# Counting two blocks of nodes with one pass over the edges, in the first stage of a graph network kernel

## The chip, the cores and the metric

The kernel runs on one core of a Trainium2 chip. The metric is the device time of one execution in microseconds (us), the median of several. Its engines are TensorE (PE, with its weight loads as PEld), VectorE (DVE), ScalarE (ACT), GpSimd (POOL) and SyncE (SP). Each runs its own instruction queue, and they wait for each other on semaphores.

## The reference

The reference is four graph layers over the same 400,000 edges between 12,500 nodes. Each layer normalises the node rows, gathers rows by edge, and adds the messages up by one end of the edge:

```python
h = relu(layernorm(x));  x = x + relu(segment_sum((h @ W0[r])[src, type] * w, dst))          # layer 0
h = relu(layernorm(x));  x = x + update(h, segment_sum(relu([h[src], e64] @ M + b), dst))    # layer 1
h = relu(layernorm(x));  x = x + segment_sum((h @ W2[r])[src, type], dst)                    # layer 2
h = relu(layernorm(x));  x = x + mlp_norm(h + segment_sum(h[dst] + e16 @ We + be, src))      # layer 3
```

Nothing in it asks for an order of the edges. The kernel needs one: it sorts edges by blocks of 128 nodes, by destination for three layers and by source for the last. To know where each block begins, it must first count the edges of each block.

## The kernel before

The 12,500 nodes make NB = 98 blocks of 128. The 400,000 edges lie on 128 partitions, COLS = 3125 per partition. The kernel is a chain of ten stages with a barrier of all engines between any two (`end_stage`). The first stage, `starts_stage`, is the only one that the change touches. It finds, for each of the 98 destination blocks and 98 source blocks, where the block's edges begin. Its work:

- SyncE loads `src` and `dst` (`ints`, `key`). VectorE shifts both by 7 bits (lines 289 and 293) and writes the block numbers as bf16 into `keys`. There the two kinds alternate, so that `k3[:, :, 0]` is the destination block and `k3[:, :, 1]` the source block, each at a step of two elements.
- VectorE then fills small constant tiles (lines 298 to 311), among them `pad`, and SyncE writes 212 filler tiles to `rec` and `rec2` (lines 224 and 227), on its own queue.
- The counts per partition go to `cnt`, 196 wide. VectorE counts destination blocks 0 to DV - 1 = 85 directly, one pass over the 3125 edges for each (line 314): compare with the block's number, and add the ones up in the accumulator output. After each pass it waits for its own semaphore.
- ScalarE counts the rest by signs. One pass (line 247) sums the sign of `number of the block - key` shifted by a half, and the difference of two neighbouring sums is twice a count. It makes 98 passes for the source blocks, then 12 for destination blocks 86 to 97 (line 253), each waiting for the one before.
- VectorE goes on with the remainders of the node numbers (lines 317 to 323, six operations over all edges), waits for ScalarE's last sum, takes the differences (lines 326 and 327), halves them (line 328) and releases TensorE (`s_cnt`).
- TensorE sums the counts over partitions (lines 263 and 264), VectorE makes tile numbers of them, and at `s_last` SyncE and ScalarE each write 49 padding tiles (line 211) through their queues. The stage ends when those have landed. Meanwhile VectorE and TensorE compute the lists `blks` and `blkd` (lines 360 to 366).

The next stage, `record_stage`, begins behind the barrier.

Of the kernel before, what the change touches and what calls it, by code (L numbers as in the profile page):

```python
# [14 lines left out]
BF16 = mybir.dt.bfloat16  # L15
I32 = mybir.dt.int32
ALU = mybir.AluOpType
ACT = mybir.ActivationFunctionType
# [8 lines left out]
NB = -(-N // P)  # L27
COLS = E // P
# [36 lines left out]
KEYS = 2  # L65
# [2 lines left out]
EQ = 3 * P  # L68
EW = EQ + CG * FE
WIDE = KEYS * NB  # L70
DV = 86
SPARE = -(-NB // G)


def peeled(engine, count, step):

    step(0)
    with engine.Fori(1, count) as i:
        step(i)


def wait_earlier(engine, semaphore, value):

    if not isinstance(value, int) or value > 0:
        engine.wait_ge(semaphore, value)
# [30 lines left out]
def build(nc, a, out):  # L116
    ctx = ExitStack()
    with ctx:
# [22 lines left out]
        keys, off, padq = b.take(COLS, BF16), b.take(WIDE), b.take(QT * ROW // 2, BF16)  # L141
        lasts = b.take(2 * NB, I32)
        starts_stage(nc, sem, a, Buffers(arena, b.at), psum, iotaf, ident, iotab, identb, ones, pidx, epsc, blkd, blks,
                     ints, flts, srcl, keys, off, padq, lasts, rec, rec2)
        sem.end_stage()
# [29 lines left out]
def starts_stage(nc, sem, a, b, psum, iotaf, ident, iotab, identb, ones, pidx, epsc, blkd, blks,  # L175
# [3 lines left out]

    key, tmp = b.take(COLS, I32), b.take(COLS, I32)  # L180
    eq, junk = (b.take(COLS // 2 + 1, BF16)[:, 0:COLS] for _ in range(2))
    tri, nums, nbias = b.take(P), b.take(NB + 1), b.take(NB + 1)
    gd, gs = b.take(NB + 1), b.take(NB + 1)
    cnt, tiles, incl, ti, wide = (b.take(WIDE) for _ in range(5))
    ti = ti.bitcast(I32)
    col = [b.take(1) for _ in range(KEYS)]
# [12 lines left out]
    s_v, s_ks, s_kd, s_hist, s_sign, s_cnt, s_pre, s_last, s_tge, s_tps, s_blk = (  # L199
        sem("r_" + n) for n in ("v", "ks", "kd", "hist", "sign", "cnt", "pre", "last", "tge", "tps", "blk"))  # L200
    k3 = keys.rearrange("p (t k) -> p t k", k=KEYS)
    TC, QC = ([(c, min(512, n - c)) for c in range(0, n, 512)] for n in (TILES, QUADS))

    def pad_last_tiles(engine, lo, hi, at):

        with engine.Fori(lo, hi) as i:
            engine.load(at, last[0:1, bass.ds(i * 2, 2)])
            group = engine.snap(at[0], min_val=0, max_val=GROUPS + SPARE - 1)
            place = engine.snap(at[1], min_val=0, max_val=G - 1)
            tile = rect[bass.ds(group, 1), bass.ds(place, 1)].rearrange("g j p w -> (g j p) w")  # L210
            engine.dma_start(tile, pad).then_inc(s_filled, 16)

    with nc.Block() as block:
        @block.sync
        def _(sp):
            sp.dma_start(ints[:, COLS:2 * COLS], a["src"]).then_inc(s_src, 16)
            sp.dma_start(key, a["dst"]).then_inc(s_dst, 16)
            sp.dma_start(flts[:, 0:COLS], a["w"]).then_inc(s_rest, 16)
            sp.dma_start(ints[:, 0:COLS], a["type"]).then_inc(s_rest, 16)

            sp.wait_ge(s_pad, 1)
            with sp.Fori(FULL, GROUPS) as g:
                for j in range(G):
                    sp.dma_start(rect[bass.ds(g, 1), j:j + 1].rearrange("g j p w -> (g j p) w"), pad).then_inc(s_fill, 16)
            with sp.Fori(FULL, GROUPS2) as g:
                for j in range(G // QT):
                    sp.dma_start(quads[bass.ds(g, 1), j:j + 1].rearrange("g j p w -> (g j p) w"), padq).then_inc(s_fill, 16)
            sp.wait_ge(s_fill, FILLS * 16)
            at = [sp.alloc_register(f"r_last{k}") for k in range(2)]
            sp.wait_ge(s_last, 1)  # L230
            pad_last_tiles(sp, 0, NB // 2, at)
            sp.wait_ge(s_filled, NB * 16)
# [8 lines left out]
        @block.scalar  # L241
        def _(act):
            act.wait_ge(s_ks, 1)

            def source_signs(i):
                wait_earlier(act, s_sign, i)
                nc.scalar.activation(junk, k3[:, :, 1], ACT.Sign, bias=nbias[:, bass.ds(i, 1)],
                                     accum_out=gs[:, bass.ds(i, 1)]).then_inc(s_sign, 1)
            peeled(act, NB, source_signs)
            act.wait_ge(s_kd, 1)  # L250
            with act.Fori(DV, NB) as i:
                act.wait_ge(s_sign, i + (NB - DV))
                nc.scalar.activation(junk, k3[:, :, 0], ACT.Sign, bias=nbias[:, bass.ds(i, 1)],
                                     accum_out=gd[:, bass.ds(i, 1)]).then_inc(s_sign, 1)
            at = [act.alloc_register(f"r_lasta{k}") for k in range(2)]
            act.wait_ge(s_last, 1)
            act.wait_ge(s_fill, FILLS * 16)
            pad_last_tiles(act, NB // 2, NB, at)
# [18 lines left out]
        def _(dve):  # L277
            chain = [0]

            def link(ins):  # L280
                chain[0] += 1
                ins.then_inc(s_v, 1)
                dve.wait_ge(s_v, chain[0])

            v = nc.vector
# [18 lines left out]
            link(v.memset(epsc, EPS))  # L304
            link(v.memset(ones, 1.0))
            link(v.memset(gs[:, NB:NB + 1], -float(COLS)))
            link(v.memset(gd[:, NB:NB + 1], -float(COLS)))
            link(v.tensor_scalar(ident, iotaf, pidx, None, ALU.is_equal))
            link(v.tensor_copy(iotab, iotaf))
            link(v.tensor_copy(identb, ident))  # L310
            link(v.tensor_scalar(tri, iotaf, pidx, None, ALU.is_gt))
            dve.wait_ge(s_kd, 1)
            with dve.Fori(0, DV) as i:
                v.tensor_scalar(eq, k3[:, :, 0], nums[:, bass.ds(i, 1)], None, ALU.is_equal, ALU.add,
                                accum_out=cnt[:, bass.ds(i, 1)]).then_inc(s_hist, 1)
                dve.wait_ge(s_hist, i + 1)
            link(v.tensor_scalar(tmp, key, P - 1, None, ALU.bitwise_and))
            link(v.tensor_copy(flts[:, COLS:2 * COLS], tmp))
            link(v.tensor_scalar(tmp, ints[:, COLS:2 * COLS], P - 1, None, ALU.bitwise_and))
# [2 lines left out]
            link(v.tensor_scalar(tmp, ints[:, COLS:2 * COLS], 4, None, ALU.logical_shift_left))  # L322
            link(v.tensor_tensor(ints[:, 0:COLS], tmp, ints[:, 0:COLS], ALU.bitwise_or))

            dve.wait_ge(s_sign, NB + NB - DV)
            link(v.tensor_tensor(cnt[:, DV:NB], gd[:, DV:NB], gd[:, DV + 1:NB + 1], ALU.subtract))
            link(v.tensor_tensor(cnt[:, NB:WIDE], gs[:, 0:NB], gs[:, 1:NB + 1], ALU.subtract))
            v.tensor_scalar(cnt[:, DV:WIDE], cnt[:, DV:WIDE], 0.5, None, ALU.mult).then_inc(s_cnt, 1)
            dve.wait_ge(s_pre, 1)

            quantum = (P, QT * P)
# [1126 lines left out]
```

## Time and profile before

| what | value |
|---|---|
| median of 3 runs | 23065.33 us (23064.5 to 23086.5) |
| the profiled execution | 23081.41 us |
| its span, first to last instruction | 23079.6 us |
| busy in the span: GpSimd, VectorE, TensorE, ScalarE | 67%, 44%, 41%, 8% |
| VectorE's counting passes (line 314) | 86, 298.6 us busy |
| ScalarE's counting passes (lines 247 and 253) | 110, 2.902 us each |
| first instruction of the second stage | at 465.1 us |

The busy shares are means over ten stages. The change lies in the first, which takes 2% of the span. There GpSimd is idle but for 3.5 us, so the shares of the whole say nothing of this stage.

### The profile page before, as it was taken

The numbers are of one execution on the slowest core, as the hardware profiler recorded it, in microseconds if no ns is written. First come the engines' busy times: TensorE is split into PE (matmuls) and PEld (weight loads), VectorE is DVE, ScalarE is ACT, GpSimd is POOL, SyncE is SP. The second block draws the span as 40 slices with busy tenths as digits, with TensorE's granted clock in tenths as the row PEclk, the third lists the DMA queues.
The fourth block names the chain that finished last, engine by engine and source line by source line (L and its number), as shares of the span: only waits on it lengthen the run. The fifth ranks groups of instructions, "written<-read, shape, count | busy, mean of one in ns | idle before, by whom it ended". The sixth has DMA issues, their size and how long they took to land. (4 is left out here: it accounts for less than half of the span.)

```text
span 23079.6 us, 208272 instructions
## 1 busy us (share of the span) xinstructions
PE 9435.0 (41%) x48147; PEld 7205.3 (31%) x48150; DVE 10242.7 (44%) x25180; ACT 1861.0 (8%) x4901; POOL 15540.0 (67%) x16453
## 2 busy tenths in 40 slices
PE   0777776433333334333333543333332222222366
PEld 0333333233333333333333333333331111111254
DVE  7777777544444443333333432222224333333473
ACT  5000000000000000000000100000001111111100
POOL 0777777777777767777777267777776777777400
PEclk8555555555555555555555655555555555555686
DMA  2333332222222232222222322222223222222462
GB/s 86 99 98 98 99 98 81 70 64 61 64 61 62 63 45 62 61 63 61 61 61 61 72 89 63 61 64 61 64 61 64 83 83 83 83 82 82 131 222 69
DMA packets 1005113, 1785.47 MB, mean 77 GB/s; under 512 B 352294, under 2 KB 461123, under 8 KB 1004534
## 3 DMA queue, kind: packets, MB, share of 16 engines
q1 hardware_dynamic: 484294, 1127.71, 15.6%
q0 software_dynamic: 513696, 654.80, 12.5%
q10 hardware_dynamic: 7056, 2.21, 0.0%
q8 instruction: 24, 0.39, 0.0%
q14 instruction: 43, 0.35, 0.0%
HBM read 1279.37 MB, written 510.79 MB: 78 GB/s over the span
## 5 line engine op out<-in xcount | busy, mean ns | idle before, releaser
L1018 PE MATMUL psum<-arena 128*128 128x64 f32 x19392 | 4447.2, 424 | 7925.5 <-DMA arena<-table,arena 4589.6
L919 POOL DMA_INDIRECT arena<-table,arena x6464 | 6104.2, 944 | 2005.8 <-issue 1932.5
L1018 PEld LDWEIGHTS psum<-arena 128*128 128x128 f32 x19392 | 4226.9, 330 | 8146.0 <-issue 6208.1
L970 DVE TENSOR_TENSOR arena<-arena,psum 128x64 f32 x9696 | 2150.5, 222 | 6333.8 <-PE psum L1018 4413.8
L687 POOL DMA_INDIRECT rec<-arena x3125 | 3001.1, 960 | 1476.0 <-issue 949.0
L1123 POOL DMA_INDIRECT rec<-arena x3232 | 3180.4, 984 | 1093.8 <-issue 971.1
L919 POOL DMA_INDIRECT arena<-ptable,arena x3232 | 3147.6, 974 | 997.8 <-issue 984.3
L464 PE MATMUL psum<-arena 128*128 128x196 bf16 (+1 forms) x4375 | 1378.5, 429 | 1262.4 <-DVE arena L595 1262.3
L1142 DVE TENSOR_TENSOR arena<-psum,arena 128x1024 bf16<-128x1024 f32 x404 | 494.6, 1224 | 2716.2 <-DMA arena<-rec 2716.2
L1190 PE MATMUL psum<-arena 128*128 128x128 bf16 x3232 | 418.0, 311 | 2526.8 <-DVE arena L1142 2526.8
L1190 PEld LDWEIGHTS psum<-arena 128*128 128x128 bf16 x3232 | 312.7, 141 | 2673.6 <-DVE arena L1142 2345.0
L595 DVE TENSOR_TENSOR arena<-psum,arena 128x392 f32<-128x392 f32 x1875 | 918.2, 490 | 365.1 <-PE psum L464 241.0
L464 PEld LDWEIGHTS psum<-arena 128*128 128x128 bf16 x4375 | 366.8, 115 | 2188.1 <-DVE arena L595 1812.4
L949 DVE TENSOR_TENSOR arena<-psum,arena 128x1024 f32<-128x1024 f32 x808 | 984.1, 1218 | 25.7 <-issue 22.6
L976 DVE TENSOR_TENSOR arena<-arena 128x512 f32<-128x512 f32 x404 | 287.4, 711 | 1580.5 <-DMA arena<-ptable,arena 1580.5
L1201 PE MATMUL psum<-arena 128*128 x3232 | 589.6, 363 | 643.0 <-DVE arena L1150 552.8
L1291 PE MATMUL psum<-arena 128*128 128x81 bf16 x10560 | 604.2, 228 | 471.8 <-DVE arena L1259 465.8
L600 DVE TENSOR_REDUCE arena<-arena 128x10 f32<-128x980 f32 x625 | 734.0, 1174 | 21.6
L587 DVE TENSOR_TENSOR arena<-psum,arena 128x980 bf16<-128x980 f32 x625 | 729.2, 1167 | 0.0
L1150 DVE CAST arena<-psum 128x1536 bf16<-128x1536 f32 x404 | 707.3, 1751 | 5.9 <-PE psum L1201 5.6
L1291 PEld LDWEIGHTS psum<-arena 128*128 128x128 bf16 x10560 | 538.3, 116 | 537.9 <-issue 444.3
L775 ACT ACTIVATE arena<-arena 128x98 f32<-128x98 f32 x3 | 1.1, 377 | 8307.4 <-DVE arena L709 8307.4
(189 smaller groups left out, 10301.8 us busy)
## 6 DMA issues: line engine op xcount, KB each, us to landing
arena<-rec SPq DMA_DIRECT2D x303, 1408.0 KB
arena<-rec SPq DMA_DIRECT2D x440, 488.0 KB, 4.4
arena<-in_edge SPq DMA_DIRECT2D x625, 232.0 KB, 2.6
arena<-rec SPq DMA_DIRECT2D x404, 352.0 KB, 3.3
arena<-table,arena POOLq DMA_INDIRECT x6464, 2.4
rec<-arena POOLq DMA_INDIRECT x6357, 2.3
table<-arena SPq DMA_DIRECT2D x196, 512.0 KB
arena<-ptable,arena POOLq DMA_INDIRECT x3232, 2.4
```

What stands on the lines that cost most here:

```text
L464: return nc.tensor.matmul(to, identb, one_hots, start=False, stop=False, skip_group_check=True)
L587: v.tensor_tensor(buf[g].rearrange("p (t w) -> p t w", w=NB), numsw, keyw, ALU.is_equal).then_inc(s_hot, 1)
L595: v.tensor_tensor(prod[g][:, 2 * n * WIDE:2 * n * WIDE + w], run[:, 0:w], buf[g][:, 2 * n * WIDE:2 * n * WIDE + w], ALU.mult).then_inc(s_s ...
L600: v.tensor_reduce(posf[:, g * CG * KEYS:(g + 1) * CG * KEYS], prod[g].rearrange("p (t w) -> p t w", w=NB), AX.X, ALU.add).then_inc(s_red, 1)
L687: nc.gpsimd.indirect_dma_start(rec, bass.IndirectOffsetOnAxis(ap=stage[g][:, j:j + 1], axis=0), recs[g][:, j * RW:(j + 1) * RW], None).the ...
L919: nc.gpsimd.indirect_dma_start(rows[q][:, j * D:(j + 1) * D], None, tab, bass.IndirectOffsetOnAxis(ap=idx[:, j, field:field + 1], axis=0)) ...
L949: v.tensor_tensor(ones, iotas, lanes, ALU.is_equal).then_inc(s_hot[q], 1)
L970: v.tensor_tensor(block_sum, block_sum, ps[q % SB][:, j * D:(j + 1) * D], ALU.add).then_inc(s_add[j], 1)
L1018: last = nc.tensor.matmul(ps[q % SB][:, j * D:(j + 1) * D], hot[q % SB][:, j * P:(j + 1) * P], rows[q][:, j * D:(j + 1) * D], start=True, ...
L1123: nc.gpsimd.indirect_dma_start(rec2, bass.IndirectOffsetOnAxis(ap=idx[:, j, R_SLOT:R_SLOT + 1], axis=0), rows[q][:, j * ROW:(j + 1) * ROW] ...
L1190: last = nc.tensor.transpose(ps_t[q % 2][:, j * P:(j + 1) * P], hot[q][:, j * P:(j + 1) * P], identb)
L1291: last = nc.tensor.matmul(ps[q % RING][j // QT], hot[q][:, j * P:(j + 1) * P], rows[q][:, at:at + MW], start=j % QT == 0 and k == 0, stop= ...
```

## The change

The number of a block is split into half of it (`half` = node number shifted by 8, 0 to 48) and its lowest bit. A tile `unit` holds 1 for an even block and 4096 for an odd one, computed as `4095 * (block - 2 * half) + 1`. One pass then compares `half` with the number of a pair of blocks, multiplies by `unit` and sums. As no partition has more than 3125 edges, the sum holds the even block's count in its lowest 12 bits and the odd block's above them; all values stay under 2^24 and are exact in float32.

VectorE makes 49 such passes for the 98 destination blocks and SD = 7 for source blocks 0 to 13, 56 in place of 86. Each is now a `scalar_tensor_tensor` with two tensor inputs, both bf16 and without gaps, in place of a `tensor_scalar` with one input at a step of two. Before the passes it computes `half` and `unit` for both kinds of key: four operations over all edges for each, eight in all. Behind them five small operations over 56 columns take the sums apart into `cnt`. ScalarE counts only source blocks 14 to 97: 84 passes in place of 110. The tile `gd`, its memset and its subtraction go. The waits of the passes on themselves stay, as do the work on the remainders and all behind it.

```diff
+PAIRS = NB // 2
+SD = 7
+COUNT = 1 << 12
-            peeled(act, NB, source_signs)
-            act.wait_ge(s_kd, 1)
-            with act.Fori(DV, NB) as i:
-                act.wait_ge(s_sign, i + (NB - DV))
-                nc.scalar.activation(junk, k3[:, :, 0], ACT.Sign, bias=nbias[:, bass.ds(i, 1)],
-                                     accum_out=gd[:, bass.ds(i, 1)]).then_inc(s_sign, 1)
+            source_signs(2 * SD)
+            with act.Fori(2 * SD + 1, NB) as i:
+                act.wait_ge(s_sign, i - 2 * SD)
+                source_signs(i)
...
-            link(v.memset(gd[:, NB:NB + 1], -float(COLS)))
...
-            with dve.Fori(0, DV) as i:
-                v.tensor_scalar(eq, k3[:, :, 0], nums[:, bass.ds(i, 1)], None, ALU.is_equal, ALU.add,
-                                accum_out=cnt[:, bass.ds(i, 1)]).then_inc(s_hist, 1)
-                dve.wait_ge(s_hist, i + 1)
+            for k, keyi in ((0, key), (1, ints[:, COLS:2 * COLS])):
+                link(v.tensor_scalar(tmp, keyi, 8, None, ALU.arith_shift_right))
+                link(v.tensor_copy(half[k], tmp))
+                link(v.scalar_tensor_tensor(unit[k], half[k], -2.0, k3[:, :, k], ALU.mult, ALU.add))
+                link(v.tensor_scalar(unit[k], unit[k], float(COUNT - 1), 1.0, ALU.mult, ALU.add))
+            for k, pairs, at in ((0, PAIRS, 0), (1, SD, PAIRS)):
+                with dve.Fori(0, pairs) as i:
+                    v.scalar_tensor_tensor(eq, half[k], nums[:, bass.ds(i, 1)], unit[k], ALU.is_equal, ALU.mult,
+                                           accum_out=both[:, bass.ds(i + at, 1)]).then_inc(s_hist, 1)
+                    dve.wait_ge(s_hist, i + (at + 1))
+            link(v.tensor_copy(two, both))
+            link(v.tensor_scalar(low, two, COUNT - 1, None, ALU.bitwise_and))
+            link(v.tensor_scalar(two, two, COUNT.bit_length() - 1, None, ALU.arith_shift_right))
+            counted = cnt[:, 0:2 * (PAIRS + SD)].rearrange("p (b o) -> p b o", o=2)
+            link(v.tensor_copy(counted[:, :, 0:1], low.rearrange("p (b o) -> p b o", o=1)))
+            link(v.tensor_copy(counted[:, :, 1:2], two.rearrange("p (b o) -> p b o", o=1)))
...
-            dve.wait_ge(s_sign, NB + NB - DV)
-            link(v.tensor_tensor(cnt[:, DV:NB], gd[:, DV:NB], gd[:, DV + 1:NB + 1], ALU.subtract))
-            link(v.tensor_tensor(cnt[:, NB:WIDE], gs[:, 0:NB], gs[:, 1:NB + 1], ALU.subtract))
-            v.tensor_scalar(cnt[:, DV:WIDE], cnt[:, DV:WIDE], 0.5, None, ALU.mult).then_inc(s_cnt, 1)
+            dve.wait_ge(s_sign, NB - 2 * SD)
+            link(v.tensor_tensor(cnt[:, NB + 2 * SD:WIDE], gs[:, 2 * SD:NB], gs[:, 2 * SD + 1:NB + 1], ALU.subtract))
+            v.tensor_scalar(cnt[:, NB + 2 * SD:WIDE], cnt[:, NB + 2 * SD:WIDE], 0.5, None, ALU.mult).then_inc(s_cnt, 1)
```

## Rows read from the trace of the kernel before

**Rows 1.** The page: the span, and the busy time of each engine in it.

```profile
span 23079.6 us, 208272 instructions
...
PE 9435.0 (41%) x48147; PEld 7205.3 (31%) x48150; DVE 10242.7 (44%) x25180; ACT 1861.0 (8%) x4901; POOL 15540.0 (67%) x16453
```

**Rows 2.** Busy time by stretch of the first stage (us), clock, DMA share, GB/s.

```profile
core 0: us, PE busy (x) PEld busy (x) DVE busy (x) ACT busy (x) POOL busy (x), PEclk, DMA share, GB/s
100.00:150.00 50.00, 0.00 (x0) 0.00 (x0) 43.59 (x25) 47.63 (x32) 0.00 (x0) 1.00 0.97 348
150.00:200.00 50.00, 0.00 (x0) 0.00 (x0) 43.05 (x27) 47.47 (x31) 0.00 (x0) 1.00 0.00 0
...
340.00:360.00 20.00, 0.00 (x0) 0.00 (x0) 17.32 (x11) 17.12 (x12) 0.00 (x0) 1.00 0.00 0
420.00:440.00 20.00, 0.00 (x0) 0.00 (x0) 0.00 (x0) 0.00 (x0) 0.00 (x0) 0.50 0.21 54
```

**Rows 3.** ScalarE's source passes and VectorE's passes, by line (duration in ns).

```profile
L247 ACT ACTIVATE arena<-arena x98: 2901/2902/2904, 11.5 to 317.1; 128x3125 bf16<-128x3125 bf16 x98
...
L314 DVE TENSOR_SCALAR_CACHE_REDUCE arena<-arena x86: 3471/3473/3475, 18.7 to 359.7; 128x3125 bf16<-128x3125 bf16 x86
```

**Rows 4.** Timeline where the counting begins: start, duration in us, engine, operation.

```profile
11.50 2.90 ACT L247 ACTIVATE arena<-arena 128x3125 bf16<-128x3125 bf16 x1 [9.48 <-DVE arena L290]
...
17.96 0.28 DVE L311 TENSOR_SCALAR arena<-arena 128x128 f32<-128x128 f32 x1
18.68 3.47 DVE L314 TENSOR_SCALAR_CACHE_REDUCE arena<-arena 128x3125 bf16<-128x3125 bf16 x1 [0.43 <-DVE arena L311]
...
22.74 3.47 DVE L314 TENSOR_SCALAR_CACHE_REDUCE arena<-arena 128x3125 bf16<-128x3125 bf16 x1 [0.58 <-DVE arena L314]
```

**Rows 5.** Timeline where the counting ends.

```profile
354.92 2.90 ACT L253 ACTIVATE arena<-arena 128x3125 bf16<-128x3125 bf16 x1 [0.16 <-ACT arena L253]
...
357.73 0.19 ACT L253 ACTIVATION_READ_ACCUMULATOR arena<-arena  x1
...
363.06 0.08 DVE L314 DVE_READ_ACCUMULATOR arena<-arena  x1
363.35 1.79 DVE L317 TENSOR_SCALAR arena<-arena 128x3125 int32<-128x3125 int32 x1 [0.21 <-DVE arena L314]
...
372.46 3.41 DVE L323 TENSOR_TENSOR arena<-arena 128x3125 int32<-128x3125 int32 x1
375.91 0.17 DVE L326 TENSOR_TENSOR arena<-arena 128x12 f32<-128x12 f32 x1
...
376.41 0.22 DVE L328 TENSOR_SCALAR arena<-arena 128x110 f32<-128x110 f32 x1
...
376.68 0.69 PE L263 MATMUL psum<-arena 128*128 128x196 f32 x1 [376.68 <-DVE arena L328]
```

**Rows 6.** Timeline from the counts to the next stage.

```profile
383.88 78.80 ACTq L211 DMA_DIRECT2D rec<-arena  x49
...
395.49 0.92 DVE L366 TENSOR_SCALAR arena<-psum 128x512 int32<-128x512 f32 x2 [0.17 <-PE psum L274]
...
465.10 0.26 DVE L651 COPY psum<-arena 128x98 f32<-128x98 f32 x1 [68.69 <-PEq L101]
```

**Rows 7.** SyncE's queue: the second set of fills.

```profile
78.25 67.67 SPq L227 DMA_DIRECT2D rec<-arena  x100
```

**Rows 8.** VectorE by line and shape: count, busy us, mean ns.

```profile
L1259 DVE TENSOR_SCALAR arena<-arena 128x128 bf16<-128x128 bf16 x3520 | 609.9, 248 | 15.9 <-issue 15.9
...
L713 DVE SCALAR_TENSOR_TENSOR arena<-arena 128x6272 f32<-128x6272 f32 x4 | 26.8, 6692 | 0.1
...
L308 DVE TENSOR_SCALAR arena<-arena 128x128 f32<-128x128 f32 x1 | 0.3, 287 | 0.0
...
L343 DVE SCALAR_TENSOR_TENSOR arena<-arena 128x98 f32<-128x98 f32 x1 | 0.3, 260 | 0.0
...
L326 DVE TENSOR_TENSOR arena<-arena 128x12 f32<-128x12 f32 x1 | 0.2, 171 | 0.0
```

More of the change, by code:

```diff
@@ L70 @@
 WIDE = KEYS * NB
-DV = 86
+PAIRS = NB // 2
+SD = 7
+COUNT = 1 << 12
+assert NB % 2 == 0 and COLS < COUNT
 SPARE = -(-NB // G)
@@ L181, in starts_stage @@
     eq, junk = (b.take(COLS // 2 + 1, BF16)[:, 0:COLS] for _ in range(2))
+    half, unit = ([b.take(COLS // 2 + 1, BF16)[:, 0:COLS] for _ in range(KEYS)] for _ in range(2))
+    both, two, low = b.take(PAIRS + SD), b.take(PAIRS + SD, I32), b.take(PAIRS + SD, I32)
     tri, nums, nbias = b.take(P), b.take(NB + 1), b.take(NB + 1)
-    gd, gs = b.take(NB + 1), b.take(NB + 1)
+    gs = b.take(NB + 1)
     cnt, tiles, incl, ti, wide = (b.take(WIDE) for _ in range(5))
@@ L245, in source_signs @@
             def source_signs(i):
-                wait_earlier(act, s_sign, i)
                 nc.scalar.activation(junk, k3[:, :, 1], ACT.Sign, bias=nbias[:, bass.ds(i, 1)],
                                      accum_out=gs[:, bass.ds(i, 1)]).then_inc(s_sign, 1)
-            peeled(act, NB, source_signs)
-            act.wait_ge(s_kd, 1)
-            with act.Fori(DV, NB) as i:
-                act.wait_ge(s_sign, i + (NB - DV))
-                nc.scalar.activation(junk, k3[:, :, 0], ACT.Sign, bias=nbias[:, bass.ds(i, 1)],
-                                     accum_out=gd[:, bass.ds(i, 1)]).then_inc(s_sign, 1)
+            source_signs(2 * SD)
+            with act.Fori(2 * SD + 1, NB) as i:
+                act.wait_ge(s_sign, i - 2 * SD)
+                source_signs(i)
             at = [act.alloc_register(f"r_lasta{k}") for k in range(2)]
```

## The prediction

> **What bounds the kernel now.** I read the page first, then the busy times by stretch, the lines of the two counting loops, the timeline at both ends of the counting, and last the shapes that come nearest to the new instructions. The page [rows 1] gives GpSimd 67% of the span, and a reader could stop there and say that VectorE's work counts for nothing. The stretches show why that is wrong here: in the first stage GpSimd and TensorE do nothing, while VectorE is busy 17.3 us and ScalarE 17.1 to 19 us of every 20 [rows 2]. The counting is the only work. What DMA there is, the filler tiles, is over before 150 us: SyncE issues the last of them by 78.25 + 67.67 = 145.9 us [rows 7], and from 150 us on the queues are silent [rows 2].
>
> Two loops run side by side. ScalarE begins at 11.50 us [rows 4] and makes 98 source passes whose starts lie (317.1 - 11.5) / 97 = 3.15 us apart [rows 3]; 12 more at the same step end at 357.9 us [rows 5]. VectorE begins at 18.68 us and makes 86 passes, (359.6 - 18.7) / 85 = 4.01 us apart, of which 3.47 us is the operation and 0.54 us the read of the accumulator, the wait on itself and the loop [rows 3, 4]. It ends at 363.1 us. Then it does the remainders until 375.9 us, takes the differences and releases TensorE at 376.63 us (376.41 + 0.22) [rows 5]. So VectorE sets the end and ScalarE had 18 us to spare. Both steps are the same inside the stretch with heavy DMA and behind it: 43.6 and 43.1 us busy in 50 [rows 2].
>
> Behind the counts comes a tail that nothing shortens. Padding tiles are issued from 383.88 us, for 78.80 us, and the next stage starts at 465.10 us [rows 6]: 88.5 us from the counts to the next stage, set by small VectorE steps and two DMA queues. All engines wait at the barrier, so what the counting saves moves the whole rest forward.
>
> **ScalarE's part.** It loses 26 passes: 84 remain. The first starts at the same 11.50 us, as nothing before it changes. The last starts at 11.50 + 83 x 3.15 = 273.0 and ends, with its accumulator read (3.0 us in all [rows 5]), at 276.0 us.
>
> **VectorE's part, step by step.**
> - Removed in front: one memset of a single column, about 0.1 us. The new work starts at 18.1 us in place of the loop; `keys` has been written for long by then.
> - Added in front, for each kind of key: a shift of int32 (1.79, as L317), a cast to bf16 (1.79, for which I take the shift's duration, 2 bytes being no slower to write), a two-input operation over 3125 elements, and a scaling of bf16. For the two-input one the nearest rows are L323, int32, 3.41 us [rows 5], and L713, the same kind of operation on float32, 6.69 us for 6272 elements, so one element in (6692 - 3412) / 3147 = 1.04 ns [rows 5, 8]. I take 3.41. For the scaling, `tensor_scalar` on 128 columns takes 287 ns from float32 to float32 and 248 ns from bf16 to bf16 [rows 8]; 39 ns less in 128 elements is 0.30 ns each, or 0.95 less than 1.79 over 3125. I take 0.9; above it stands 3.47, the row of one element at a time. The four with gaps of 0.03 give 8.0 us, both kinds 16.0 (at most 21.1). The loop can begin at about 34.1 us and its first pass at 34.6.
> - The passes: 56. This is the step on which all hangs, as no row of before shows `scalar_tensor_tensor` with bf16 inputs or with an accumulator output. Without an accumulator it takes one element in 1.04 ns with float32 (L713), the same as a two-input operation (L323), which gives 3.41 us. The accumulator made the old pass 3.47 in place of that. I take 3.47, and the old 0.54 around it, so 4.01 us: 56 x 4.01 = 224.6. The second of the two loops starts anew for 0.4. The passes end at 259.6 us. Below: an operation with both inputs in 2 bytes, without gaps, might take two elements at a time, 1.79 us as the shift does, and a step of 2.33; then VectorE ends 94 us earlier and waits for ScalarE. Above: half the rate, (2 x 3125 x 1.042 + 155) ns = 6.67 us.
> - The taking apart: five small operations, each 0.17 to 0.26 us like L326 and L343 [rows 8], 1.2 us with gaps. The passes' sums are done at 260.8.
> - The remainders, unchanged: 363.35 to 375.88, 12.5 us [rows 5]. VectorE is at its wait for ScalarE at about 273.4 us.
>
> **The sum.** ScalarE is last now, at 276.0, by 2.6 us. Then one subtraction over 84 columns (0.26) and the halving (0.22), with gaps and the hand-over (0.2): the counts are released at 276.7 us. The subtraction over 12 columns is gone. 376.6 - 276.7 = 99.9 us, call it 100. The tail of 88.5 us goes with it. Nothing is queued behind the moved wait on VectorE but this chain; SyncE and ScalarE wait for `s_last` behind it, and the fillers that they also wait for have landed 130 us before. The tail's own queues see the same load: no fillers then, as now. The granted clock is 1.00 in the counting and 0.50 at 420 us [rows 2]; only the handful of matmuls of this stage lie before that, some 2 us of them in the chain to `s_last`, so if they came at the lower clock it would cost about 2 us.
>
> The profiled execution took 23081.41 us, 1.8 us more than its span; less 100 that is 22981. It lies 16 us above the median, within the 22 us of the three runs. The metric is the median: 23065.3 - 100 = **22965 us**, 0.43% less. About 0.2% (46 us) is what a measurement of this kernel can tell from no change.
>
> **A rule against the change.** L713 takes one float32 element of each of two inputs in 1.04 ns [rows 8], with no accumulator. The Trainium skill, "Vector Engine (DVE) Microarchitecture Reference", section "Points that are easy to get wrong", says that an operation of this very shape runs at half throughput when its two inputs in SBUF are not bf16, because no read port is left for the accumulator. L713 doesn't agree for the case without an accumulator; by the rule's letter bf16 inputs escape it, and the sum stays. If the halving held with the accumulator whatever the type, it would be the first rival below.
>
> **Rivals.**
> - *The new pass runs at half rate (slower).* Place: each of the 56 passes. Price: 6.67 + 0.54 = 7.21 us, 404 us in all; the preparation with its two operations at 6.67 takes 22.5 and ends at 41. The counts come at 41 + 404 + 1 + 12.5 + 1 = 460 us, 83 us later than now: 23148 us. Against it are L713 and L323, which read two 4-byte inputs at full rate, and L314, which accumulates at full rate; for it only that no row has both at once. It decides from the point where the preparation, 56 steps and 14 us reach 376: a step of (376 - 34.6 - 14.6) / 56 = 5.84 us, or a pass of 5.3. I give it 0.07.
> - *VectorE stays last by a little more per pass.* The two loops meet at a step of 4.01 + 2.6 / 56 = 4.06 us. Each tenth of a microsecond above that costs 5.6 us. A pass of 3.6 to 3.9, say because the two-input form takes the accumulator or the register's number more slowly, gives 22972 to 22990 us, still clearly faster. 0.12, for up to half of the gain lost.
> - *The scaling or the cast is slow.* At most 5.1 us more in front, so the end moves by 2.5 us: inside the forecast.
> - *The gain doesn't arrive at the end (same).* It would need something in the tail that keeps to its own time, such as the padding writes. For it: they take 79 us of the 88.5. Against: they are issued only at `s_last`, and their queues have been empty for over 200 us before. About 23060 us, 0.03.
>
> **How the numbers follow.** ScalarE's end is the forecast, 0.78: here the VectorE pass may be anything up to 3.52 us, also two elements at a time, and the time is the same, 22965, as ScalarE's 84 passes can't be shortened by it. Its own range is 22948 to 22982, from the spread of 22 us that the three runs show, laid to both sides, less a little. The range of 8 in 10 takes in most of the second case: 22947 to 22992. Faster holds the forecast and the second case: 0.90. Same 0.03, slower 0.07.
>
> **What would show it.** In the profile after: ScalarE's last pass ends near 276 us with 84 passes 3.15 us apart; VectorE's 56 passes of 3.4 to 3.5 us, 4.0 us apart, end near 260; VectorE's wait in front of its subtraction ends on ScalarE and is about 2 to 3 us long; the first matmul comes near 276.7 and the second stage at 365. The eight operations in front take 16 us. If the passes read near 1.8 us, the step on their rate is wrong and the time right, with VectorE waiting for ScalarE for 90 us or more. If they read near 6.7 us, the forecast is wrong in sign. If the second stage starts 100 us earlier and the total doesn't follow, the cause lies behind the barrier.

## The result

The changed kernel takes 22962.19 us (median of 5, 22956.11 to 22993.52) against 23064.5 us before (median of 5, 23056.11 to 23086.5): 102 us less. The ratio is 0.9959 with a 95% interval of 0.9949 to 0.997. The forecast was 22965 us, in a range of 22947 to 22992. (The ratio on record is not the quotient of the two medians, here 0.9956; the quotient lies inside its interval.)

The page of the changed kernel, its span and busy times, stands against [rows 1]:

```profile
span 22991.7 us, 207917 instructions
...
PE 9432.7 (41%) x48147; PEld 7206.5 (31%) x48150; DVE 10159.5 (44%) x25131; ACT 1783.1 (8%) x4849; POOL 15546.8 (68%) x16453
```

The profiled execution took 22993.5 us and is the slowest of the five, so its span is only 88 us shorter than that of before. Where the 100 us came from is seen in the first stage. First the lines of the two counting loops (count, duration in ns as least/median/most, first and last start in us), which answer to [rows 3]:

```profile
L251 ACT ACTIVATE arena<-arena x84: 2901/2902/2904, 11.7 to 273.7; 128x3125 bf16<-128x3125 bf16 x84
```

```profile
L322 DVE SCALAR_TENSOR_TENSOR arena<-arena x56: 3476/3477/3480, 35.0 to 254.8; 128x3125 bf16<-128x3125 bf16 x56
```

ScalarE makes 84 passes of the same 2.902 us, (273.67 - 11.68) / 83 = 3.16 us apart. VectorE makes 56 passes of 3.48 us, (254.78 - 34.95) / 55 = 4.00 us apart. Next the timeline where the counting begins, which answers to [rows 4]:

```profile
11.68 2.90 ACT L251 ACTIVATE arena<-arena 128x3125 bf16<-128x3125 bf16 x1 [9.66 <-DVE arena L292]
...
18.36 1.79 DVE L316 TENSOR_SCALAR arena<-arena 128x3125 int32<-128x3125 int32 x1
20.18 1.79 DVE L317 CAST arena<-arena 128x3125 bf16<-128x3125 int32 x1
...
22.01 3.42 DVE L318 SCALAR_TENSOR_TENSOR arena<-arena 128x3125 bf16<-128x3125 bf16 x1
...
25.46 0.98 DVE L319 TENSOR_SCALAR arena<-arena 128x3125 bf16<-128x3125 bf16 x1
...
34.95 3.48 DVE L322 SCALAR_TENSOR_TENSOR arena<-arena 128x3125 bf16<-128x3125 bf16 x1 [0.40 <-DVE arena L319]
```

The new operations stand between 18.36 and 34.95 us: a shift, a cast, the two-input operation and the scaling, then the same for the other kind of key. Then the timeline where the counting ends, which answers to [rows 5]:

```profile
258.18 0.08 DVE L322 DVE_READ_ACCUMULATOR arena<-arena  x1
258.47 0.19 DVE L325 CAST arena<-arena 128x56 int32<-128x56 f32 x1 [0.21 <-DVE arena L322]
...
259.61 1.79 DVE L331 TENSOR_SCALAR arena<-arena 128x3125 int32<-128x3125 int32 x1
...
268.72 3.42 DVE L337 TENSOR_TENSOR arena<-arena 128x3125 int32<-128x3125 int32 x1
...
273.67 2.90 ACT L251 ACTIVATE arena<-arena 128x3125 bf16<-128x3125 bf16 x1 [0.16 <-ACT arena L251]
276.48 0.19 ACT L251 ACTIVATION_READ_ACCUMULATOR arena<-arena  x1
276.76 0.25 DVE L340 TENSOR_TENSOR arena<-arena 128x84 f32<-128x84 f32 x1 [4.63 <-ACT arena L251]
277.05 0.20 DVE L341 TENSOR_SCALAR arena<-arena 128x84 f32<-128x84 f32 x1
...
277.31 1.02 PE L265 MATMUL psum<-arena 128*128 128x196 f32 x2 [277.31 <-DVE arena L341]
```

Read it from the bottom. TensorE starts at 277.31 us, released by the halving. The subtraction at 276.76 us had waited 4.63 us for ScalarE, whose last accumulator read begins at 276.48. VectorE had ended its passes at 258.26 us, had taken the sums apart by 259.6 and done the remainders by 272.1. So the counts are released at 277.25 us, against 376.63 before. The tail, which answers to [rows 6]:

```profile
284.50 79.02 ACTq L216 DMA_DIRECT2D rec<-arena  x49
...
296.73 0.92 DVE L379 TENSOR_SCALAR arena<-psum 128x512 int32<-128x512 f32 x2 [0.36 <-PE psum L276]
...
365.94 0.26 DVE L664 COPY psum<-arena 128x98 f32<-128x98 f32 x1 [68.30 <-PEq L104]
```

The second stage begins at 365.94 us in place of 465.10: 99.2 us earlier. The tail took 88.7 us, as before (88.5).

### The profile page after: what moved, and what is told of

It is laid out like the page before. It is cut to its first block and busy times, and to the rows that moved or that the text cites. A ratio compares the mean times of both kernels' runs of the same rounds, so it can differ in the third digit from the quotient of the medians.

```text
span 22991.7 us, 207917 instructions
## 1 busy us (share of the span) xinstructions
PE 9432.7 (41%) x48147; PEld 7206.5 (31%) x48150; DVE 10159.5 (44%) x25131; ACT 1783.1 (8%) x4849; POOL 15546.8 (68%) x16453
## 3 DMA queue, kind: packets, MB, share of 16 engines
q0 software_dynamic: 513696, 654.80, 12.5%
```

## The experiments

Each was measured beside the kernel before on the same chip. `e_pair_only`, `e_sd0`, `e_f32`, `e_contig`, `e_again`, `e_all` and `e_all3` ran on two chips where the kernel before takes 26980 and 26976 us in place of 23065. The first stage of the changed kernel takes the same time there within 0.6 us (it ends at 365.4 and 365.9 us), so events of this stage can be compared across the chips; totals can't. Where the 3900 us lie is told in the last section.

Seven kernels were executed once each, and their totals are:

| kernel | total, us | kernel before on that chip, us |
|---|---|---|
| `e_pair_only` | 26995.5 | 26980.5 (13 runs) |
| `e_f32` | 26896.8 | 26980.5 |
| `e_contig` | 27023.4 | 26980.5 |
| `e_sd8` | 22961.1 | 23083.8 (1 run) |
| `e_rem` | 22986.1 | 23083.8 |
| `e_two` | 22948.0 | 23083.8 |
| `e_pads` | 22973.4 | 23083.8 |

These totals do not follow the start of the second stage: `e_pads` starts it 25 us before `e_sd8` and took 12 us longer. What is said below of these seven is shown for the first stage; a gain in the total is not shown for any of them over the changed kernel.

**`e_pair_only`: pairs on VectorE alone.** In the kernel before, the 86 one-block passes become 43 pair passes; ScalarE keeps its 110.

```diff
-            with dve.Fori(0, DV) as i:
-                v.tensor_scalar(eq, k3[:, :, 0], nums[...], None, ALU.is_equal, ALU.add, accum_out=cnt[...])
+            with dve.Fori(0, DV // 2) as i:
+                v.scalar_tensor_tensor(eq, half, nums[...], unit, ALU.is_equal, ALU.mult, accum_out=both[...])
```

> Pairing alone: VectorE counts destination blocks 0 to 85 in 43 passes of two blocks, ScalarE keeps its 110 passes. Theory (the later of two loops sets the end, and the changed kernel gains only because 26 of ScalarE's passes went too): VectorE is through near 213 us, ScalarE's last pass still ends near 358 us, the counts are released near 359 us, and the second stage starts near 447 us: 18 us earlier than before, not 99. Rival (VectorE's passes alone carry the gain): the second stage starts near 366 us.

The timeline of this kernel, at the end of VectorE's remainders and at the end of the counting:

```profile
208.43 3.42 DVE L336 TENSOR_TENSOR arena<-arena 128x3125 int32<-128x3125 int32 x1
...
357.54 0.19 ACT L256 ACTIVATION_READ_ACCUMULATOR arena<-arena  x1
357.83 0.17 DVE L339 TENSOR_TENSOR arena<-arena 128x12 f32<-128x12 f32 x1 [145.98 <-ACT arena L256]
```

VectorE is done at 211.85 us and then waits 145.98 us for ScalarE. The second stage starts at 446.81 us, 18 us before the kernel before. Pairing alone is worth a fifth of the change; the rest comes from the 26 passes that ScalarE no longer makes. VectorE's saved time had to be given work. The one time taken, 26995.5 us, can't show 18 us.

**`e_sd0` and `e_sd0_again`: the seven source pairs back to ScalarE.**

```diff
-SD = 7
+SD = 0
-            for k, pairs, at in ((0, PAIRS, 0), (1, SD, PAIRS)):
+            for k, pairs, at in ((0, PAIRS, 0),):
```

> The seven pair passes over source blocks go back to ScalarE, which makes 98 passes again. Theory: ScalarE ends 14 x 3.16 = 44 us later than in the changed kernel, near 321 us; the first matmul comes near 321.5 and the second stage starts near 410 us; the time follows one to one, 55 us under the kernel before, near 23009. Rival (the gain doesn't pass the barrier one to one): the stage moves and the time doesn't.

TensorE's first matmul came at 320.6 us, as expected. The second stage started at 413.14, 3 us later than expected, since the padding was issued over 82.7 us and not 78.9:

```profile
327.93 82.73 SPq L216 DMA_DIRECT2D rec<-arena  x49
```

The time was a miss: 26962.25 us (10 runs) against 26980.52 (13 runs), 18 us less where 52 had been gained in the stage. The ratio is 0.9995, 0.9986 to 1.0005, which is at most 38 us less, so the 52 lie outside the interval. So the same kernel was measured again.

> The kernel with SD 0 once more, since its median lay 18 us under the kernel before where 52 us of the stage's start had been gained. Theory (the gain passes the barrier one to one, and the stages behind scatter by tens of microseconds): the second stage starts near 413 us again and the median lies 30 to 70 us under the kernel before. Rival (something behind the barrier takes two thirds of it back in this kernel): the median lies 10 to 25 us under it again.

TensorE's timeline in that run, the first matmul of the counts and the first of the second stage:

```profile
320.50 1.02 PE L265 MATMUL psum<-arena 128*128 128x196 f32 x2 [320.50 <-DVE arena L341]
...
412.89 0.99 PE L541 MATMUL psum<-arena 128*128 128x392 f32 x1 [73.67 <-PEq L104]
```

23019.9 us (11 runs) against 23068.97 (15 runs): 49 us less, ratio 0.9979, 0.997 to 0.9988, where the second stage starts 465.1 - 412.9 = 52 us earlier. On this chip, one where the kernel before takes 23069 us, the gain arrives whole. Why the slower chip's median showed 18 isn't settled. Its stages behind the barrier scatter more (last section), but the interval there takes in such scatter and still leaves the 52 out.

**`e_f32`: float32 inputs, the rule against the change.** The tiles `half` and `unit` are float32.

```diff
-    half, unit = ([b.take(COLS // 2 + 1, BF16)[:, 0:COLS] for _ in range(KEYS)] for _ in range(2))
+    half, unit = [flts[:, COLS:2 * COLS], b.take(COLS)], [srcl, b.take(COLS)]
```

> The tiles half and unit are float32 in place of bf16, all else stays. The rule of the Trainium skill, Vector Engine (DVE) Microarchitecture Reference, on two inputs that are not bf16 with an accumulator: a pass takes twice as long, about 6.7 us, VectorE ends near 453 us and the second stage starts near 543 us. Rival (one element of each input in 1.04 ns whatever the type, as L713 had it without an accumulator): a pass stays at 3.48 us; the scaling of unit grows from 0.98 to 1.79 us twice, hidden behind ScalarE, and the second stage starts at 366 us as in the changed kernel.

VectorE by line and shape (count, busy us, mean ns):

```profile
L322 DVE SCALAR_TENSOR_TENSOR arena<-arena 128x3125 bf16<-128x3125 f32 x56 | 194.8, 3478 | 28.8 <-DVE arena L322 28.4 <-DVE arena L319 0.4
...
L318 DVE SCALAR_TENSOR_TENSOR arena<-arena 128x3125 f32<-128x3125 f32 x2 | 6.8, 3416 | 0.1
```

A pass with two float32 inputs and an accumulator takes 3478 ns, as with bf16 (3477). The Trainium skill, "Vector Engine (DVE) Microarchitecture Reference", section "Points that are easy to get wrong", gives two inputs in SBUF that are not bf16 half the throughput. That doesn't show here. The scaling of `unit` (line 319) rose to 1.79 us, as expected, in the time that VectorE would have waited for ScalarE. Nothing else moves, and the second stage starts at 365.7 us. The first rival of the prediction had no ground in either type.

**`e_contig`: the old pass on keys without gaps.** The kernel before, with a copy of the destination keys.

```diff
+            link(v.tensor_copy(flat, k3[:, :, 0]))
-                v.tensor_scalar(eq, k3[:, :, 0], nums[...], None, ALU.is_equal, ALU.add, accum_out=cnt[...])
+                v.tensor_scalar(eq, flat, nums[...], None, ALU.is_equal, ALU.add, accum_out=cnt[...])
```

> The kernel before, whose one-block passes read a copy of the destination keys without gaps (one copy of 3125 elements more in front). Theory: the pass with an accumulator takes one element at a time whatever the step, so it stays at 3.47 us and the copy's 1 to 2 us are all that is added: second stage near 467 us. Rival (the step of two elements alone kept the old pass slow): a pass falls to 1.8 us or 1.0 us, VectorE ends near 220 us or earlier, and the second stage starts near 447 us behind ScalarE, which would mean that the pairing was not needed for it.

```profile
L316 DVE TENSOR_SCALAR_CACHE_REDUCE arena<-arena 128x3125 bf16<-128x3125 bf16 x86 | 298.6, 3472 | 45.9 <-DVE arena L316 45.5 <-DVE arena L314 0.4
...
L314 DVE COPY arena<-arena 128x3125 bf16<-128x3125 bf16 x1 | 1.8, 1792 | 0.0
```

The old pass takes 3472 ns with and without gaps (3473 in [rows 3]), and its copy 1.79 us. So bf16 without gaps buys nothing once an accumulator is asked for, and fewer passes were the only way to less VectorE time. The second stage started at 464.1 us: the counts came 1.6 us later, and the padding was issued over 76.2 us in place of 78.8.

**`e_sd8`: one pair more for VectorE.**

```diff
-SD = 7
+SD = 8
```

> One more pair of source blocks goes to VectorE (57 passes), two passes fewer remain on ScalarE (82). Theory (two loops, the later one sets the end, and in the changed kernel ScalarE is later by 4.6 us): ScalarE ends near 270.4 us, VectorE reaches its subtraction 4.0 us later than in the changed kernel, near 276.1 us, and waits for nothing there; the second stage starts within 1 us of 366 us, so the split of the changed kernel is at its optimum. Rival (ScalarE alone sets the end): the second stage starts 6.3 us earlier, near 359.6 us.

```profile
269.76 0.18 ACT L251 ACTIVATION_READ_ACCUMULATOR arena<-arena  x1
...
272.28 3.41 DVE L337 TENSOR_TENSOR arena<-arena 128x3125 int32<-128x3125 int32 x1
275.73 0.24 DVE L340 TENSOR_TENSOR arena<-arena 128x82 f32<-128x82 f32 x1
```

Now ScalarE is done first, at 269.9 us, and the subtraction follows the remainders at once, at 275.73: VectorE sets the end. The second stage starts at 364.7 us, 1.2 us before the changed kernel's, of which 1.0 us lies in the counts. The loops cross between SD 7 and 8, and what sets the end is the later of the two. So SD 7 is near the best split but 8 is 1 us better; the expectation had called 7 the optimum. One total says nothing of 1 us.

**`e_rem`: the remainders behind the list.** The six operations over all edges move to the end of VectorE's program; SD is 9.

```diff
-SD = 7
+SD = 9
-            link(v.tensor_scalar(tmp, key, P - 1, None, ALU.bitwise_and))
...
             for j, (c, w) in enumerate(TC):
...
+            link(v.tensor_scalar(tmp, key, P - 1, None, ALU.bitwise_and))
...
             dve.wait_ge(s_blk, len(TC) + 1)
```

> The six operations on the remainders (12.5 us) move behind the list of block numbers, where VectorE stood idle for 68 us beside the padding writes, and SD is 9 (58 passes on VectorE, 80 on ScalarE). Theory: ScalarE ends near 264 us, VectorE near 267.6, the second stage starts near 357 us, 9 us earlier than in the changed kernel; the moved work ends near 301 us and delays nothing. Rival (the padding writes are slowed by VectorE's work, or the moved work delays the second stage): it starts at 366 us or later.

VectorE's timeline, the subtraction, the last of the moved operations and the first of the second stage:

```profile
266.98 0.24 DVE L332 TENSOR_TENSOR arena<-arena 128x80 f32<-128x80 f32 x1
...
295.77 3.41 DVE L379 TENSOR_TENSOR arena<-arena 128x3125 int32<-128x3125 int32 x1
355.72 0.26 DVE L663 COPY psum<-arena 128x98 f32<-128x98 f32 x1 [56.54 <-PEq L104]
```

The counts come 9.8 us earlier than in the changed kernel, the moved work ends at 299.2 us, and the second stage starts at 355.7: 10.2 us gained. The padding writes covered the moved work in full: they took 78.5 us, as without it. The edit has two parts, the moved work and SD 9; without the second, ScalarE would still end at 276.7.

**`e_two`: the wait one pass behind.** Both loops write to two throw-away tiles in turn.

```diff
-                nc.scalar.activation(junk, k3[:, :, 1], ...)
+                nc.scalar.activation(junk[k], k3[:, :, 1], ...)
-                act.wait_ge(s_sign, i - 2 * SD)
+                    act.wait_ge(s_sign, i * 2 + (k - 2 * SD - 1))
-                    dve.wait_ge(s_hist, i + (at + 1))
+                        dve.wait_ge(s_hist, i * 2 + (at + q - 1))
```

> Both counting loops write their throw-away output to two tiles in turn and wait for the pass before the last in place of the last one; SD stays 7. Theory (the 0.52 us gap of VectorE and the 0.16 us gap of ScalarE are the round trip of the semaphore): VectorE's step falls from 4.00 to about 3.6 us, ScalarE's from 3.16 to about 3.0 us; ScalarE ends near 264 us and the second stage starts near 353 us. Rival (the gaps are the loop's and the registers' instructions): the steps stay within 0.05 us and the second stage starts at 366 us.

VectorE's timeline at the start of the passes, and ScalarE's at their end:

```profile
37.75 0.08 DVE L324 DVE_READ_ACCUMULATOR arena<-arena 128x1 f32 x1
37.75 3.47 DVE L324 SCALAR_TENSOR_TENSOR arena<-arena 128x3125 bf16<-128x3125 bf16 x1
41.14 0.08 DVE L324 DVE_READ_ACCUMULATOR arena<-arena 128x1 f32 x1
41.14 3.47 DVE L324 SCALAR_TENSOR_TENSOR arena<-arena 128x3125 bf16<-128x3125 bf16 x1
```

```profile
247.74 0.18 ACT L251 ACTIVATION_READ_ACCUMULATOR arena<-arena  x1
247.83 2.89 ACT L251 ACTIVATE arena<-arena 128x3125 bf16<-128x3125 bf16 x1
250.62 0.18 ACT L251 ACTIVATION_READ_ACCUMULATOR arena<-arena  x1
```

The steps fell further than expected: VectorE's from 4.00 to 3.40 us and ScalarE's from 3.16 to 2.88, as the read of one pass's accumulator now lies under the start of the next pass. Both start at 37.75 us in the rows. ScalarE ends at 253.7, VectorE waits 15 us for it, and the second stage starts at 346.0 us: 19.9 us gained. The counts came 23.0 us earlier; the padding took 82.0 us in place of 78.9 and gave 3 of them back. The gap in both loops, paid 140 times, was the wait on the loop's own last pass, together with whatever had to run behind that wait. The edit also makes two passes per turn of the loop, and a loop of two passes with the old wait was not tried. But in the new kernel a step across the loop's turn takes the same 3.40 us as one inside it, so the turn itself costs nothing once no pass waits for the one before.

**`e_pads`: 14 registers at a time.**

```diff
-        with engine.Fori(lo, hi) as i:
-            engine.load(at, last[0:1, bass.ds(i * 2, 2)])
+        with engine.Fori(lo // LB, hi // LB) as i:
+            engine.load(at, last[0:1, bass.ds(i * (2 * LB), 2 * LB)])
+            for j in range(LB):
```

> The 49 padding writes of each of two queues are issued in 7 turns that load 14 registers at once and issue 7 writes, in place of 49 turns with a load of 2 registers and one write. Theory (of the 1.61 us per write about 1 us is the load of the registers and what hangs on it, as the fillers, without such a load, are issued every 0.55 to 0.68 us): 49 writes take about 40 us in place of 79, and the second stage starts near 327 us, which shows that the tail behind the counts is the padding. Rival (a write of this shape takes 1.6 us to issue): nothing moves, 366 us.

```profile
286.55 51.06 SPq L218 DMA_DIRECT2D rec<-arena  x49
```

The direction was right and the size was not: 49 writes take 51.1 us (1.04 each) in place of 78.9 (1.61), where 40 had been expected. The second stage starts at 340.0 us, 25.9 us earlier. So the tail is the padding, and about a third of it was the 42 turns that went, each with its register load (0.66 us a turn; load and turn were not taken apart).

**`e_again`, `e_all`, `e_all3`: the version that beats both.** `e_again` is the changed kernel unaltered, for comparison on one chip. `e_all` has the edits of `e_rem`, `e_two` and `e_pads`, with SD 10. `e_all3` sends 28 of the 98 padding writes through GpSimd's queue, with a semaphore of its own, and 35 through each of the others.

> The changed kernel once more, unaltered, on the same chip as the two kernels below, so that they can be compared with it. Theory: the second stage starts near 366 us and the time lies 99 us under the kernel before.

> All three edits of the experiments in one kernel: two throw-away tiles in turn, the remainders behind the list, padding in 7 turns of 7; SD is 10, as the steps are now 3.40 us (VectorE, 59 passes) and 2.88 us (ScalarE, 78 passes). Theory: ScalarE ends near 236.6 us, VectorE near 236; the counts are released near 237.4 us, the padding takes 53 us, and the second stage starts near 300 us, 66 us before the changed kernel's, the time near 165 us under the kernel before. Rival (the edits share a gain, for instance the moved work now stretches the shorter tail): the second stage starts past 310 us.

> As the kernel with all three edits, but the padding goes out on three queues: 35 writes each on SyncE's and ScalarE's, 28 on GpSimd's. Theory (each queue issues a write in 1.04 us whatever the others do): the padding takes 37 us in place of 53 and the second stage starts near 285 us; past that VectorE's moved work, which ends near 270 us, would be next. Rival (GpSimd's queue makes its own descriptors and is slower than 1.3 us per write, or the three queues hinder each other): the second stage starts at 300 us or later.

The second stage of `e_again` starts here:

```profile
365.42 0.27 DVE L664 COPY psum<-arena 128x98 f32<-128x98 f32 x1 [68.51 <-PEq L104]
```

In `e_all` (VectorE: the subtraction, the last remainder operation, the first of the second stage):

```profile
236.85 0.24 DVE L347 TENSOR_TENSOR arena<-arena 128x78 f32<-128x78 f32 x1 [0.65 <-ACT arena L253]
...
266.32 3.42 DVE L394 TENSOR_TENSOR arena<-arena 128x3125 int32<-128x3125 int32 x1
294.90 0.26 DVE L678 COPY psum<-arena 128x98 f32<-128x98 f32 x1 [25.17 <-PEq L105]
```

In `e_all3` (the three queues' writes; GpSimd's begin in the last row but one):

```profile
244.98 32.38 ACTq L219 DMA_DIRECT2D rec<-arena  x35
...
246.76 32.32 SPq L219 DMA_DIRECT2D rec<-arena  x35
...
247.65 1.97 POOL L219 DMA_DIRECT2D rec<-arena  x3 [243.35 <-issue]
...
281.24 0.26 DVE L684 COPY psum<-arena 128x98 f32<-128x98 f32 x1 [11.70 <-PEq L105]
```

| kernel | second stage starts, us | median, us | ratio to before (interval) |
|---|---|---|---|
| before (same chip, 10 runs) | not profiled there | 26975.54 | 1 |
| `e_again` | 365.4 | 26883.72 | 0.9965 (0.9953 to 0.9977) |
| `e_all` | 294.9 | 26838.54 | 0.9939 (0.9926 to 0.9953) |
| `e_all3` | 281.2 | 26810.57 | 0.9933 (0.992 to 0.9947) |

The changed kernel's gain is there again, 92 us in the medians. `e_all` ended its counts at 237.3 us as expected and its padding took 45.6 us where 53 was expected, so its second stage starts 5 us sooner than that. Why the same writes took 51.1 us in `e_pads` wasn't found. In total, 165 us less than before had been expected; the medians differ by 137, and the ratio's interval is 127 to 200 us. `e_all3` issues 35 writes in 32.4 us on each of two queues (37 expected), 0.92 us each, as in `e_all` (0.93). GpSimd's queue needs 27.4 us for its 28, 0.98 each. So the three queues don't hinder each other here, and the second stage starts at 281.2 us (285 expected).

Both beat the changed kernel. `e_all3` does so by 73 us in the medians, 84 us in the start of the second stage, and its interval lies clear. `e_all` does so by 45 us in the medians where its second stage starts 70.5 us earlier; its interval just touches that of `e_again`. `e_all` and `e_all3` can't be told apart by their intervals, only by the stage's start.

## Why the prediction was right

- *What sets the end of the counting.* Right. ScalarE is last in the changed kernel, by 4.6 us (2.6 forecast); `e_pair_only` and `e_sd0` moved the end by ScalarE's passes alone, and `e_sd8` put VectorE last.
- *ScalarE's 84 passes.* Forecast to end at 276.0 us, ended at 276.67: the first began 0.18 us later and a step measured 3.16 in place of 3.15.
- *VectorE's passes.* Forecast to end at 259.6 us, ended at 258.26. The first began 0.35 us late, but the sum had counted the gap behind the last pass and 0.4 for the start of the second loop; the longest of the 55 gaps is 0.6 us, so no such start shows. With the remainders VectorE was ready 1.3 us before the forecast and ScalarE 0.7 behind it, hence 4.6 us of waiting in place of 2.6.
- *The work in front of VectorE's passes.* Forecast 16.0 us, measured 16.2 (18.36 to 34.56). The scaling took 0.98 us, where 0.9 had been worked out from two shapes of 128 columns, with 3.47 as the bound.
- *The price on which all hung.* A two-input pass with an accumulator measured 3.48 us, 3.47 taken; the step 4.00, 4.01 taken. The lower bound (two elements at a time) and the upper one (half rate) both fell away, the upper also for float32 inputs.
- *The taking apart and the remainders.* 1.1 and 12.5 us, forecast 1.2 and 12.5.
- *The release of the counts.* 277.25 us, forecast 276.7; saved 99.4, forecast 99.9.
- *The tail passes the gain on.* Right: 88.7 us against 88.5. The second stage starts 99.2 us earlier, and the medians differ by 102, with an interval of 69 to 118 us from the ratio. That the medians meet the forecast to 3 us is in part luck, as the five runs spread over 37 us. So is the tail's 0.2 us: it came to 92.5 us in `e_sd0` and 91.8 in `e_two`, whose edits don't touch it. The two profiled executions differ by 88 only. Of the 11 us missing, 1.7 lie in GpSimd's scatter of records and 8.1 in the stretch behind it (13037 us against 13029 before), which scatters by 32 us between kernels with the same program there.
- *The second rival's price.* 22972 to 22990 us leaves out the 2.6 us that VectorE had to spare; with them a pass of 3.6 to 3.9 us gives 22970 to 22987. The range stated would hold either.
- *The bound of the clock.* The chain's first two matmuls (line 265) take 1.02 us together, as those of line 263 did before, and the granted clock reads 1.00 (2.4 GHz) in the 2 us around them in both kernels. So the 2 us set aside were not needed.

## What to carry to other kernels

Read the stage and not the page: GpSimd is busy 68% of the changed kernel's span, and 3.5 us in the stage that the change sped up. Where two engines share out like work, a cheaper pass on one is worth its saving only if passes move over from the other until both end together; here that split was four fifths of the gain. And look at what a loop waits for: a wait on its own last pass, for the sake of a tile that nobody reads, cost 0.60 us on VectorE and 0.28 us on ScalarE each time, and a second tile, with two passes per turn, removed it.

## What the runs showed of the hardware

- A pass with an accumulator took the same 3.47 to 3.48 us for 3125 elements in all forms tried: one bf16 input with gaps or without, two bf16 inputs, two float32 inputs. Without an accumulator a scaling of 3125 bf16 values took 0.98 us and a copy from every second element 1.79.
- The read of the accumulator costs nothing on VectorE or ScalarE when the next pass needn't wait: in `e_two` a step was 3.40 us on VectorE where the pass alone reads 3.47, and 2.88 us on ScalarE where it reads 2.89.
- The issue of the 49 padding writes took a time that goes with the kernel and not with the chip: 78.5 to 79.0 us in most kernels that keep the old loop, 76.2 in `e_contig`, 82.0 in `e_two`, and 82.7 in `e_sd0` on both kinds of chip, though none of these edits touches the writes. The cause wasn't found. So a start of the second stage shows a change of 4 us only with the release of the counts beside it.
- Chips ran the same program at two speeds, 23065 and 26980 us, at nearly the same granted clock of TensorE (0.526 and 0.522 for the changed kernel). The first two lines below are GpSimd's scatter of records in the second stage, of the changed kernel and of the same kernel as `e_again` (least/median/most duration in ns, first and last start):

```profile
L700 POOL DMA_INDIRECT rec<-arena x3125: 954/959/6397, 404.4 to 4382.9; - x196
```

```profile
L700 POOL DMA_INDIRECT rec<-arena x3125: 952/958/1112, 403.9 to 5266.8; - x196
```

The instruction takes the same 0.96 us, yet the writes spread over 4863 us in place of 3979. From the last record to the first message written, a stretch with the three stages that gather rows, it is 13037 and 15399 us, and the scatter of messages (the two rows below) 4165 and 4817, while the first stage, the sums by source (991 and 992 us) and the last (395 and 389) don't change. Nearly all of the 3900 us lie in the stages with indirect transfers (884 + 2362 + 652 us). What differs between these chips wasn't found.

```profile
L1136 POOL DMA_INDIRECT rec<-arena x3232: 982/984/1065, 17419.9 to 21584.6; - x191
```

```profile
L1136 POOL DMA_INDIRECT rec<-arena x3232: 980/983/1090, 20665.3 to 25482.4; - x191
```

- The same stages make the scatter between executions. The same stretch, from the last record to the first message, has the same program in all kernels here; it took 13010 to 13042 us in seven profiled executions on chips of the faster kind and 15377 to 15432 in seven of the slower. So a single execution can't show less than some 30 us here, and for that reason the first stage was read by its events.
